# DLRM tower: low parts subtracted in quarters of 256 columns, and TensorE's waits around the grams and in table 0

## What is computed

```python
e = jnp.stack([tbl_0[ids[:, 0]], ..., tbl_25[ids[:, 25]]], axis=1)          # 512 x 26 x 128
combined = jnp.concatenate((dense[:, None, :], e), axis=1)                  # 512 x 27 x 128
interactions = jnp.einsum('bfd,bgd->bfg', combined, combined)
z = jnp.concatenate((dense, interactions[:, iu, ju]), axis=1)               # iu < ju, 351 pairs
h = jnp.concatenate([z, dense], axis=1)
h = jnp.maximum(h @ W_top1 + b_top1, 0.0)                                   # 607 -> 512
h = jnp.maximum(h @ W_top2 + b_top2, 0.0)                                   # 512 -> 256
y = h @ W_top3                                                              # 256 -> 1
```

## Time and profile before

| | us |
|---|---|
| median of 3 executions | 110.19 (110.16 to 115.2) |
| the profiled execution, its own time | 109.44 |
| its span, first to last instruction | 107.6 |
| TensorE busy (matmul) | 95.0 (88%) |
| VectorE busy | 59.8 (56%) |
| ScalarE busy | 51.4 (48%) |
| GpSimd busy | 67.0 (62%) |

### The profile page before, as it was taken

How to read it: one execution, slowest core, us unless ns; L and a number is a source line. 1 busy time by engine, 2 the same in 40 slices (tenths; PEclk the granted TensorE clock), 3 DMA queues, 4 the chain that set the end, 5 groups by cost and what they waited for, 6 DMA issues and landing times.

```text
span 107.6 us, 2501 instructions
## 1 busy us (share of the span) xinstructions
PE 95.0 (88%) x989; PEld 82.4 (77%) x989; DVE 59.8 (56%) x142; ACT 51.4 (48%) x92; POOL 67.0 (62%) x73
## 2 busy tenths in 40 slices
PE   3974999999999999399999979979999969994892
PEld 3843788687786778299999869968989849992880
DVE  0238999999999999994599703122212102230033
ACT  5052846765959759756699243133123233210210
POOL 2778777788777777777777776777777300433000
PEclk9999999999999999999999999999999999999999
DMA  1769999999997665999844112344254300032000
GB/s 29 237 161 287 252 262 279 267 251 222 239 300 174 206 187 133 262 337 238 284 141 101 49 49 55 91 152 122 67 151 118 86 3 6 18 129 62 6 0 1
DMA packets 8584, 16.17 MB, mean 150 GB/s; under 512 B 4384, under 2 KB 4653, under 8 KB 8572
## 3 DMA queue, kind: packets, MB, share of 16 engines
q1 hardware_dynamic: 6459, 11.73, 40.3%
q0 software_dynamic: 2112, 4.28, 15.1%
HBM read 14.51 MB, written 1.50 MB: 149 GB/s over the span
## 4 chain that ended last, share of the span: by engine, by line
DVE 37%; PE 37%; DMA 9%; ACT 7%; issue 4%; SPq 3%; ACTq 0%
DVE onehot L588 24%; PE gram_bank L409 13%; DVE table_lo L595 11%; PE layer_bank L437 6%; PE onehot_bank L451 5%; PE onehot_bank L382 4%; DMA table_raw<-tbl 4%; DMA pair_scratch<-gram_rows 3%; PE layer_bank L423 3%; ACT table_hi L507 3%; PE transpose_bank L394 2%; ACT emb L547 2%; DMA pairs<-pair_scratch 2%; PE onehot_bank L462 2%; PE onehot_bank L378 1%
## 5 line engine op out<-in xcount | busy, mean ns | idle before, releaser
L351 POOL DMA_INDIRECT rows<-tbl,gather_ids x61 | 63.4, 1039 | 19.5 <-issue 18.3
L588 DVE TENSOR_SCALAR onehot<-match_ids,row_numbers 125x512 fp32r<-125x512 int16 (+1 forms) x96 | 37.9, 454 | 4.5 <-DMA match_ids<-onehot_ids 3.4
L378 PE MATMUL onehot_bank<-onehot,table_hi 125*128 125x512 f32 (+1 forms) x96 | 24.8, 401 | 2.1 <-DVE onehot L588 1.5
L382 PE MATMUL onehot_bank<-onehot,table_lo 125*128 125x512 f32 (+1 forms) x96 | 23.6, 389 | 0.3
L378 PEld LDWEIGHTS onehot_bank<-onehot,table_hi 125*128 125x128 f32 x96 | 17.8, 198 | 5.7 <-issue 2.2
L382 PEld LDWEIGHTS onehot_bank<-onehot,table_lo 125*128 125x128 f32 x96 | 17.8, 197 | 5.2 <-DVE table_lo L595 3.1
L507 ACT CAST table_hi<-table_raw 125x1024 fp32r<-125x1024 f32 (+1 forms) x13 | 12.8, 985 | 17.1 <-PE onehot_bank L382 8.9
L595 DVE TENSOR_TENSOR table_lo<-table_raw,layer_bank 125x512 fp32r<-125x512 f32 x24 | 16.2, 677 | 4.1 <-ACT layer_bank L514 4.1
L409 PE MATMUL gram_bank<-emb 128*54 128x54 f32 x512 | 14.2, 214 | 3.7 <-ACT emb L547 1.8
L409 PEld LDWEIGHTS gram_bank<-emb 128*54 128x54 f32 x512 | 13.5, 129 | 4.8 <-ACT emb L547 2.5
L514 ACT COPY layer_bank<-table_hi 125x512 f32<-125x512 f32 x24 | 14.3, 607 | 0.1
(11 more groups left out here) (26 smaller groups left out, 32.0 us busy)
## 6 DMA issues: line engine op xcount, KB each, us to landing
table_raw<-tbl SPq DMA_DIRECT2D x11, 448.0 KB
pair_scratch<-gram_rows SPq DMA_DIRECT2D x14, 91.1 KB
match_ids<-onehot_ids SPq DMA_DIRECT2D x2, 512.0 KB, 10.5
rows<-tbl,gather_ids POOLq DMA_INDIRECT x61, 6.1
w_pairs<-w_pairs SPq DMA_DIRECT2D x1, 702.0 KB
table_raw<-tbl SPq DMA_DIRECT2D x11, 52.0 KB
pairs<-pair_scratch SPq DMA_DIRECT2D x14, 39.0 KB
w_dense_parts<-w_dense SPq DMA_DIRECT2D x1, 512.0 KB
```

What stands on the lines that cost most here:

```text
L351: pool.indirect_dma_start(rows[:, FIRST_ROW[t] + slot - 1, :], None, tables[GATHER_TABLES[slot - 1]], bass.IndirectOffsetOnAxis(ap=gather_ ...
L378: nc.tensor.matmul(bank[:, served(i)], table_hi[:, i % 2, c * D:(c + 1) * D], onehot[:, i % 2, c, served(i)], start=(c == 0), stop=False)
L382: last = nc.tensor.matmul(bank[:, served(i)], table_lo[:, i % 2, c * D:(c + 1) * D], onehot[:, i % 2, c, served(i)], start=False, stop=(c ...
L588: nc.vector.tensor_scalar(onehot[:, i % 2, c, served(i)], match_ids[0:PARTS_1H, i, served(i)], row_numbers[:, c:c + 1], None, ALU.is_equal ...
```

## The change

- `LO_EVERY` is 2. The low part is subtracted in quarters of 256 columns, one after every second compare. Only the first quarter of a half waits for a mirror; only the last quarter of a half counts up `lo_halves`.
- In table 0 ScalarE makes the first mirror directly after casting the first half, ahead of the cast of the second half.
- `units_before_gram(t)` counts only up to the last unit that the gram reads. Gram 0 no longer waits for the copy of one-hot step 7, nor gram 1 for that of transpose (2, 1).
- ("layer2", 0) and ("dense", 1) stand ahead of ("gram", 2) instead of behind it, for all three engines.

```diff
-LO_EVERY = CHUNKS_1H // 2
+LO_EVERY = 2
...
-         ("transpose", 2, 2), ("transpose", 2, 3),
-         ("gram", 2), ("layer2", 0), ("dense", 1), ("layer3", 0), ("transpose", 3, 0),
+         ("transpose", 2, 2), ("transpose", 2, 3), ("layer2", 0), ("dense", 1),
+         ("gram", 2), ("layer3", 0), ("transpose", 3, 0),
...
 def units_before_gram(t):
-    n = sum(s in UNIT_OF for s in ORDER[:ORDER.index(("gram", t))])
-    assert all(UNIT_OF[s] < n for s in UNITS if (FIRST_TILE[s[1]] if s[0] == "onehot" else s[1]) <= t)
-    return n
+
+    needed = [s for s in UNITS if (FIRST_TILE[s[1]] if s[0] == "onehot" else s[1]) <= t]
+    assert all(ORDER.index(s) < ORDER.index(("gram", t)) for s in needed)
+    return max(UNIT_OF[s] for s in needed) + 1
...
             def mirror(i, half):
 
                 if i >= 1:
                     act.wait_ge(lo_halves, 2 * (i - 1) + half + 1)
-                act.wait_ge(hi_ready, hi_done(i))
+                act.wait_ge(hi_ready, half + 1 if i == 0 else hi_done(i))
...
-            convert_table(0)
-            mirror(0, 0)
-            mirror(0, 1)
+            for half, loaded in enumerate((table_loaded[0], second_half_loaded)):
+                convert_piece(0, table_pieces(0)[half], loaded)
+                mirror(0, half)
...
                     if c % LO_EVERY == LO_EVERY - 1:
 
-                        half = c // LO_EVERY
-                        dve.wait_ge(hi_mirrored, 2 * i + half + 1)
-                        piece = slice(half * width // 2, (half + 1) * width // 2)
-                        nc.vector.tensor_tensor(table_lo[:, i % 2, piece], table_raw[:, i % RAW, piece],
-                                                hi_mirror[half][0:PARTS_1H, :], ALU.subtract).then_inc(lo_halves, 1)
+                        half, last_of_half = divmod(c // LO_EVERY, 2)
+                        if not last_of_half:
+                            dve.wait_ge(hi_mirrored, 2 * i + half + 1)
+                        piece = slice((c + 1 - LO_EVERY) * D, (c + 1) * D)
+                        place = (c + 1 - LO_EVERY) * D - half * width // 2
+                        lo = nc.vector.tensor_tensor(table_lo[:, i % 2, piece], table_raw[:, i % RAW, piece],
+                                                     hi_mirror[half][0:PARTS_1H, place:place + LO_EVERY * D],
+                                                     ALU.subtract)
+                        if last_of_half:
+                            lo.then_inc(lo_halves, 1)
```

More of the change, by code:

```diff
@@ L500, in _, with convert_piece @@
         def _(act):
-            def convert_table(i):
[L502 to L507, removed]
+            def convert_piece(i, half, loaded):
+                act.wait_ge(loaded, 16 * len(PART_PIECES))
+                if i >= 2:
+                    act.wait_ge(unit_filled, UNIT_OF[("onehot", i - 2)] + 1)
+                nc.scalar.copy(table_hi[:, i % 2, half], table_raw[:, i % RAW, half]).then_inc(hi_ready, 1)
+            def convert_table(i):
+                convert_piece(i, slice(0, width), table_loaded[i])
             def mirror(i, half):
```

## The result

| | before | changed |
|---|---|---|
| median, us | 110.17 | 113.64 (113.5 to 114.46, 4 executions) |
| ratio | | 1.032, 95% interval 1.024 to 1.040 |
| profiled execution / its span, us | 109.44 / 107.6 | 113.78 / 111.9 |
| granted TensorE clock, mean of the profiled execution | 1.00 | 0.954 |

The change is slower by 3.2%. The forecast was 110.4 us, within 109.0 to 112.4; it was wrong, and on the side of "dear quarters", but not by their mechanism.

What follows compares the result with a forecast made beforehand. VectorE was taken to bound the tables up to table 7, TensorE the kernel from gram 1 on; +0.92 + 0.72 - 0.02 + 0.12 - 0.56 - 0.75 - 0.2 = +0.2 us on 110.19 gave 110.4 us, range 109.0 to 112.4.

Steps and rivals of the forecast that it cites:

- dear quarters: Rival: small VectorE subtractions pay 0.41 us each, 0.32 more in nine tables, 113.3 us; chance 0.20 at either price.
- The price of a quarter: VectorE's 256-column subtraction takes 0.33 us start to start, so each table costs +0.12 us, bounds 0 and +0.44.
- My +0.36: Cost per table by the skill's fixed-cost rule, with a quarter at 0.39 us; as a rival 112.6 us, counted with 0.20.
- Tables 2 to 7: VectorE sets the pace, and six tables at 0.12 us each add +0.72 us.
- keeps its own pace: Claim that GpSimd's gathers do so, so a gain beyond 0.4 to 1.6 us is cut at the last gather.
- Table 0, table 1: Table 0's earlier mirror gains 0.85 us, lost waiting for table 1's mirror; more work behind that wait makes table 1 +0.92.
- Gram 0 and table 10: Gram 0 ends 0.8 us earlier; more work behind table 10's mirror wait gives that back, leaving -0.02 us.
- Gram 1: On TensorE, it waits only for table 11's copy and starts at 62.81 instead of 63.37: -0.56 us.
- Gram 2: Layer 2 and dense cover the copy of transpose (2, 3), -0.75 us; a late copy inside the gram may go, -0.2.
- The waits dissolve: Rival: early table-0 work keeps its 0.85 us because table 1's mirror comes with it, -1.6 us, 108.6 us; chance 0.12.
- the right brake: The last gather, landing at 86.0 to 87.2 us before its transpose at 87.58, cuts gains beyond 0.4 to 1.6 us.
- The signs of being wrong: A quarter over 0.36 us, table 1's quarters before 12.8, TensorE waiting for pairs in tile 2's layer 1 or the last gather.

Runs made afterwards that it cites:

- run 7: Changed kernel with tables 1 and 10, whose first subtraction waits for its mirror, subtracted in halves: 111.02 us.
- run 9: Changed kernel with 7 calls of small unread matmuls in TensorE's idle time ahead of the last layer 1: 112.48 us, ratio 1.022.
- run 3: Changed kernel without its 61 gathers, GpSimd zeroing the gathered rows once at the start: 109.95 us, one execution.
- run 6: Changed kernel with a 128-column fill on GpSimd behind each gather: 116.05 us, one execution.
- run 11: Changed kernel with halves instead of quarters, both halves of a table subtracted behind its eighth compare: 110.53 us, one execution.
- run 4: Kernel before without its 61 gathers, GpSimd zeroing the gathered rows once: 111.6 us, one execution.
- run 2: Changed kernel with the subtraction in halves again, everything else as changed: 109.68 us, ratio 0.987 to the kernel before.
- run 10: Changed kernel with the subtraction in halves again, repeated in a later batch for a profile: 108.32 us, ratio 0.980 to the kernel before.

## Why the prediction was wrong

- **The price of a quarter** (0.33 us, table +0.12): right. 0.33 start to start; +0.12 without gathers. The rule of the Trainium skill on fixed cost ("VectorE: DVE Perf Modes", section on the TRN2 errata) comes near the durations, not the time from start to start: estimated by its figures, 0.39 us for 256 columns and 0.66 for 512, where the rows have durations of 0.405 and 0.677 and starts 0.33 and 0.60 apart, as each next instruction starts 0.07 to 0.08 before the end of the one ahead. My +0.36 took the quarter from the page and the half from the row; with both from the page it is +0.25. Neither is the measured +0.12.
- **Tables 2 to 7** (+0.72): this is the step that failed. I took a compare as 0.40 us from the old pattern and let it stand in the new one. Beside the gathers every second compare took 0.53 us instead. Tables 2 to 6 took 25.0 us (17.14 to 42.14) where I had 22.75: 2.25 us missed, and 0.3 of the same kind in table 1. The sign was in the trace of before: gathers lasted 1.08 to 1.28 us beside VectorE's compares and 0.94 once these were over, three of them filled exactly one table (4.43 us), and a compare in each table ran long. I read GpSimd's rows only for the last gather and wrote that it "keeps its own pace".
- **Table 0, table 1** (-0.85 lost in a new wait, then +0.92): right in mechanism, run 7 shows it. The data of table 1 landed 0.3 later (a cast at 11.34 instead of 11.05) and compares were held up for 0.3, so table 2 started at 17.14, not 16.53. Table 0 too ended later than forecast, at 10.89 instead of 10.33, its later compares held up as well, and so the wait in table 1 was 1.2 us, not 1.7.
- **Gram 0 and table 10** (-0.8 given back): right. 0.82 inside the gram; from the start of table 8 to that of table 11 it took 14.98 us against 14.89 before (56.54 - 41.65); with halves in table 10 the 0.8 stays.
- **Gram 1** (-0.56): right; table 11's low products to gram 1 is 0.54 shorter.
- **Gram 2** (-0.95): right in kind, too small: -1.38 from the start of gram 1 to transpose (3, 0). The late copy inside gram 2 did not return (3.53 against 3.91 us); the remaining 0.25 us were not traced to a cause.
- **TensorE's clock at the end**: the second step that failed, put at nothing: it is not in the sum, nor among the rivals. 1.5 us in the profiled execution; about 1.2 in the medians (run 9, across batches).
- **The rivals.** The side of "dear quarters" came true, by other means. "The waits dissolve" had the right brake in it, but it did not bite where I put it; its own sum has a slip, as 14.9 for the end of table 1 is 1.63 less than 16.53, and the 1.77 used belongs to 14.76.
- **The signs of being wrong.** None of the four that I named appeared: a quarter took 0.33 us, table 1 started its quarters at 13.10, and TensorE waited neither for pairs in tile 2's layer 1 nor for the last gather. What showed it was the start of table 8, 46.29 where I had 43.3.

Added up for the profiled executions: 0.2 forecast, 2.25 for tables 2 to 6, 0.6 for table 1, 0.1 for table 7, -0.4 at gram 2, 1.5 for the clock: 4.25 of the 4.3 us between the spans. Three smaller terms that nearly cancel are left out: the last wait for pairs was 0.2 us shorter, table 10 and the last layers 0.1 longer each. That the time came out on the side of "dear quarters", near its 113.3 us, is luck.

What makes GpSimd and VectorE hold each other up was not isolated. The runs show that it takes GpSimd's instructions and the wide compares (runs 3 and 6), that the subtractions, which read PSUM, keep 400 to 403 ns in the same stretch (410 without gathers), and that a hold on a gather ends within a row of eight compares (run 11). The Trainium skill ("SBUF — State Buffer", section "SBUF: two separate sides") tells of such a hold: a VectorE instruction in a mode with two ports and a GpSimd instruction share a pair of ports, and whichever starts first has it for its whole instruction, while the other is blocked. For run 3's long fill the trace agrees: the compare that met it ended 0.27 us after it. For a gather it does not: in the changed kernel one lasts from 20.70 to 21.64 us, a compare starts within it at 20.89 and the next one 0.39 later, as without gathers, and only that next one loses 0.13. So a gather's row is not one unbroken hold. In which mode the compares run, no run here shows. Why the quarters made VectorE the one that waits, and the slower gathers GpSimd again, is told by the numbers only so far: 1.13 is a little under 1.25, and VectorE was drawn up to it, while at 0.99 us (384 columns) it stayed free. In run 7 one sees it happen, cycles of 1.13 until 19.4 us and 1.25 from 20.65 on. For other ratios of the two periods no run here gives a rule.

## What to carry to other kernels

When a change alters the rhythm of an engine, look for another engine that shares something with it and has a rhythm of its own: rows whose mean differs from stretch to stretch without a change of shape (gathers of 1.18 and 0.94 us) are the sign, and a price per instruction taken from the old pattern need not hold in the new one. Where an engine waits for something that comes at a fixed time, count the work behind the wait, not ahead of it: with two compares and the dearer quarters taken back from there, run 7 had 1.3 and 0.8 us less. Test each part alone before a bundle is judged: here the parts were -1 to -2% and +4%. And look at the clock of the stretch before two totals are compared: 1.1 to 1.6 us of several differences here are one last layer at half clock.

## What the runs showed of the hardware

- A quarter and two compares, 1.13 us alone, ran at 1.25 us, exactly the period of GpSimd's gathers, for 25 us on end; a longer gather period (1.52) freed it (1.14). With compares of 384 columns the cycle was 0.99 us with gathers and without.
- A VectorE compare that began during a 6.61 us fill on GpSimd took 3.80 us instead of 0.47 and ended 0.27 us after the fill (run 3); in run 4 it took 3.70.
- The same kernel (runs 2 and 10) ran with three gathers or with two in the time of one table, 108.6 against 117.0 us in the profiled executions; in the slower one the change from three to two came at about 28 us. In the profiled executions with quarters the step of two did not occur.
- After 1.7 us of idle time TensorE worked at 1.2 GHz for 3.3 us, from about the tenth matmul after the pause on. Pauses of 1.7 to 2.3 us ahead of the last layer 1 were followed by this in seven of ten profiled executions, and that layer took 1.1 to 1.6 us longer. With 14 or 28 matmuls in the pause it came in none of four.
